# Changing the order of the first batch, and moving one tile's neighbour sums to GpSimd, in a one-core stencil and feed-forward kernel

## The reference

```python
lap_x = (yp_x[:, :, :-2] - 2.0 * y + yp_x[:, :, 2:])      # reflect padding
lap_y = (yp_y[:, :-2, :] - 2.0 * y + yp_y[:, 2:, :])
y = zX * lap_x + zY * lap_y + zR * x * (1.0 - x)          # zX, zY, zR: one number per batch
lt = y[:, 1:17, :]; even, odd = lt[:, ::2, :], lt[:, 1::2, :]
m1 = (even[:, :4, :, None] * odd[:, :4, None, :]).reshape(B, H, D)
m2 = (even[:, 4:, :, None] * odd[:, 4:, None, :]).reshape(B, D, H)
h = einsum('bsd,hd->bsh', y, W1) + scale * einsum('bsd,bhd->bsh', y, m1) + b1
h = gelu(h, approximate=False)
out = x + einsum('bsh,oh->bso', h, W2) + scale * einsum('bsh,boh->bso', h, m2) + b2
```

## Time and profile before

| | us |
|---|---|
| median of 3 runs | 1356.17 |
| lowest and highest | 1356.12, 1356.93 |
| the profiled execution, its own time | 1355.59 |
| span of the profiled execution | 1353.8 |
| TensorE busy in the span | 1341.1 (99%) |
| VectorE, ScalarE, GpSimd busy | 1046.3, 806.7, 420.7 |
| first product of layer 1 | starts at 34.10 |
| first product of layer 2 | starts at 47.63 |

### The profile page before, as it was taken

The page is one execution under the profiler, slowest core; times in us unless marked ns, Lnnn a source line. Parts: engine busy times, 40 slices in busy tenths (PEclk is TensorE's granted clock), DMA queues, the critical chain, the costliest instruction groups (busy, mean ns, idle before and its releaser), DMA issues.

```text
span 1353.8 us, 17005 instructions
## 1 busy us (share of the span) xinstructions
PE 1341.1 (99%) x5840; PEld 1096.2 (81%) x5840; DVE 1046.3 (77%) x1676; ACT 806.7 (60%) x1396; POOL 420.7 (31%) x399
## 2 busy tenths in 40 slices
PE   8899999999999999999999999999999999999999
PEld 4688888888888888888888888888888888888887
DVE  6999889957799577995889768897688967675353
ACT  3766467754676456764567555675466754666432
POOL 3453134511445014450244302453025520222100
PEclk9999999999999999999999999999999999999999
DMA  6688778867687677776778757787677866676661
GB/s 190 157 200 231 229 178 216 209 181 203 190 217 206 181 207 199 208 201 206 198 191 206 190 194 210 196 216 184 212 201 191 217 182 209 151 199 163 179 188 53
DMA packets 134070, 262.04 MB, mean 194 GB/s; under 512 B 15200, under 2 KB 23520, under 8 KB 133984
## 3 DMA queue, kind: packets, MB, share of 16 engines
q1 hardware_dynamic: 116248, 210.36, 48.6%
q0 software_dynamic: 17520, 49.81, 22.7%
q10 hardware_dynamic: 216, 0.79, 0.2%
HBM read 193.80 MB, written 67.11 MB: 193 GB/s over the span
## 4 chain that ended last, share of the span: by engine, by line
PE 93%; DVE 5%; DMA 0%; issue 0%; ACT 0%; SPq 0%; DVEq 0%; ACTq 0%
PE po L471 17%; PE po L472 17%; PE po L473 16%; PE ph L454 14%; PE ph L456 14%; PE ph L458 14%; DVE W2s L439 1%; DVE yl L299 1%; DVE W2l L446 1%; PE po L274 1%; DMA x<-in_xT_dram 0%; DVE gl L489 0%; DVE y L282 0%; DVE W1l L384 0%; DVE y L288 0%
## 5 line engine op out<-in xcount | busy, mean ns | idle before, releaser
L471 PE MATMUL po<-W2h,gh 128*128 128x512 f32 x1024 | 398.5, 389 | 2.8 <-DVE gl L489 2.8
L473 PE MATMUL po<-W2h,gl 128*128 128x512 f32 x1024 | 398.6, 389 | 0.0
L472 PE MATMUL po<-W2l,gh 128*128 128x512 f32 x1024 | 398.6, 389 | 0.0
L454 PE MATMUL ph<-yh,W1h 128*128 128x512 f32 x898 | 351.2, 391 | 2.4 <-DVE W1l L384 1.7
L456 PE MATMUL ph<-yl,W1h 128*128 128x512 f32 x898 | 349.9, 390 | 0.0
L458 PE MATMUL ph<-yh,W1l 128*128 128x512 f32 x898 | 349.8, 390 | 0.0
L489 DVE TENSOR_TENSOR gl<-ph,gh 128x512 fp32r<-128x512 f32 x256 | 175.4, 686 | 188.0 <-ACT gh L487 188.0
L471 PEld LDWEIGHTS po<-W2h,gh 128*128 128x128 f32 x1024 | 192.4, 188 | 43.2 <-DVE gl L489 3.2
L484 ACT ACTIVATE ph<-ph,b1t 128x512 f32<-128x512 f32 x256 | 167.7, 655 | 96.7 <-DVE ph L551 68.7
L473 PEld LDWEIGHTS po<-W2h,gl 128*128 128x128 f32 x1024 | 192.3, 188 | 40.2
L472 PEld LDWEIGHTS po<-W2l,gh 128*128 128x128 f32 x1024 | 192.2, 188 | 39.6
(11 more groups left out here) (91 smaller groups left out, 1285.0 us busy)
## 6 DMA issues: line engine op xcount, KB each, us to landing
W2s<-in_w_dram SPq DMA_DIRECT2D x128, 256.0 KB, 3.2
R<-in_w_dram POOLq DMA_DIRECT2D x63, 512.0 KB, 7.5
uv_scratch<-UVs SPq DMA_DIRECT2D x126, 256.0 KB, 4.4
UVs<-uv_scratch SPq DMA_DIRECT2D x126, 256.0 KB, 3.9
X<-in_xT_dram SPq DMA_DIRECT2D x56, 390.0 KB, 4.5
xr<-in_x_dram SPq DMA_DIRECT2D x16, 1024.0 KB, 5.7
xr<-in_b_dram POOLq DMA_DIRECT2D x16, 1024.0 KB, 11.3
out_dram<-xr SPq DMA_DIRECT2D x64, 256.0 KB, 2.1
```

The costliest lines, as they stand in the source:

```text
L454: e.matmul(bank[:, :], W1h[:, f, blk, wc], yh[:, s, c, :], start=first and c == 0, stop=False, skip_group_check=not first)
L471: e.matmul(po[t][:, :], gh[:, late, st], W2h[:, k, :], start=first, stop=False)
L472: e.matmul(po[t][:, :], gh[:, late, st], W2l[:, k, :], start=False, stop=False)
L473: mm = e.matmul(po[t][:, :], gl[:, late, st], W2h[:, k, :], start=False, stop=last)
```

## The change

Tile 5 joins the tiles whose neighbour sums GpSimd makes: `by_pool` gets 5, and `s0` has a fifth pair of buffers for it. The numbers of `zt` are loaded by ScalarE's queue instead of SyncE's, ahead of the natural rows; the first x tile becomes SyncE's first DMA, and the order of the other loads changes. The products of tile 0 stand ahead of the 20 small warming products (L587). `scalars(0, ...)` is planned earlier. The other lines change planned times of batch 0's first half; they move instructions, as the rows under the diff show, and change nothing in what is computed.

```diff
-            s0 = early.enter_context(nc.sbuf_tensor("s0", [128, 4, 2, 512], f32))
+            s0 = early.enter_context(nc.sbuf_tensor("s0", [128, 5, 2, 512], f32))
...
-        k_z = d_z.dma(sp, us(0.0), [(zt[:, :, :].rearrange("p b i -> p (b i)"),
+        k_z = d_z.dma(act, us(0.0), [(zt[:, :, :].rearrange("p b i -> p (b i)"),
...
-        k_N = d_N.dma(act, us(0.0), [(N, bass.AP(x.tensor, 0, [[S * D, 8], [2 * D, 8], [D, 3], [1, D]]))])
-        k_zn = d_zn.dma(sp, us(0.1), [(zn[:, 0:4], bass.AP(z.tensor, 0, [[4, 8], [0, 8], [1, 4]]))])
+        k_N = d_N.dma(act, us(0.1), [(N, bass.AP(x.tensor, 0, [[S * D, 8], [2 * D, 8], [D, 3], [1, D]]))])
+        k_zn = d_zn.dma(sp, us(0.3), [(zn[:, 0:4], bass.AP(z.tensor, 0, [[4, 8], [0, 8], [1, 4]]))])
...
-                s, pair = n, s0[:, n // 4 * 2 + n % 2, :, :]
-                load = us((0.2, 0.25, 2.1, 0.6, 1.6, 1.7, 1.5, 1.8)[n])
-                adds = us((0, 0, 8.1, 15.4, 0, 0, 6.9, 11.4)[n])
+                s, pair = n, s0[:, (0, 0, 0, 1, 0, 4, 2, 3)[n], :, :]
+                load = us((0.2, 0.6, 0.2, 0.5, 1.7, 1.8, 1.6, 1.9)[n])
+                adds = us((0, 0, 8.8, 20.6, 0, 16.7, 17.1, 17.6)[n])
...
-            by_pool = b > 0 or n in (2, 3, 6, 7)
+            by_pool = b > 0 or n in (2, 3, 5, 6, 7)
...
-                at = us((5, 9.6, 14.9, 0, 17.8, 22.3, 0, 26.8)[n])
+                at = us((-18, 10.2, 12.5, 0, 16, 21.6, 0, 28.6)[n])
...
-                return ((-43.6, 3.2, 12.5), (-49.2, 17.5, 37.3), (45.7, 64.4, 58.8), (63.9, 81.5, 89.5), (95.8, 123.1, 122.2), (120.7, 136.9, 139),
-                        (150.9, 176.2, 167.9), (173.3, 191.3, 184.4))[n]
+                return ((-48.7, -39.2, 12), (-50.1, 16.8, 57.5), (45.2, 63.9, 83.4), (77, 89.4, 89.5), (121.9, 129.5, 130), (128.5, 136.6, 142.1),
+                        (165.6, 179, 174.5), (172.6, 182.4, 211.2))[n]
...
-        scalars(0, us(10.1))
+        scalars(0, us(6.9))
```

More of the change, by code:

```diff
@@ L237, in stencil @@
             if b == 0:
-                s, pair = n, s0[:, n // 4 * 2 + n % 2, :, :]
-                load = us((0.2, 0.25, 2.1, 0.6, 1.6, 1.7, 1.5, 1.8)[n])
-                adds = us((0, 0, 8.1, 15.4, 0, 0, 6.9, 11.4)[n])
+                s, pair = n, s0[:, (0, 0, 0, 1, 0, 4, 2, 3)[n], :, :]
+                load = us((0.2, 0.6, 0.2, 0.5, 1.7, 1.8, 1.6, 1.9)[n])
+                adds = us((0, 0, 8.8, 20.6, 0, 16.7, 17.1, 17.6)[n])
                 adds = (adds, adds + 6)
-                mul, fin = us((5.7, 10, 12.2, 7.6, 17.2, 9.9, 10.9, 21.1)[n]), us((9.8, 15, 16.8, 14.7, 22.6, 28, 17.9, 28.1)[n])
-                fin = (fin, fin + 8.6, fin + 11.9)
+                mul, fin = us((3.7, 11.5, 10.8, 7.7, 23.4, 12.7, 10.9, 13.2)[n]), us((8.5, 11.5, 16.1, 6.6, 24.4, 26.8, 11.8, 25.1)[n])
+                fin = (fin, fin + 47.3, fin + 52.5)
                 free_x, free_y, prev = [], [], None
@@ L307, in operands @@
             else:
-                w0, w1_, w2_, w3, w4 = (us(21.1), us(21.6)), (us(20.8), us(24.4)), (us(37.5), us(43.7)), (us(34.8), us(39.2)), (us(38), us(45.2))
-                ws1, ws2, ws3, ws4 = us(29.1), us(34.7), us(38.4), us(38.2)
+                w0, w1_, w2_, w3, w4 = (us(21.7), us(23.1)), (us(23.8), us(24.2)), (us(45.2), us(44.2)), (us(35.8), us(39.3)), (us(45.4), us(46))
+                ws1, ws2, ws3, ws4 = us(28.9), us(34.8), us(45.6), us(37.7)
             left, hi = [ytile.at(b, n) for n in range(4)], [ytile.at(b, n) for n in range(4, 8)]
@@ L323, in operands2 @@
             T = t0(b, 0, 0)
-            w5, w6 = ((T - 14.6, T + 10.7), (T + 67.8, T + 72.5)) if b else ((110.6, 166), (125.6, 136))
+            w5, w6 = ((T - 14.6, T + 10.7), (T + 67.8, T + 72.5)) if b else ((109.9, 221.8), (124.6, 192.5))
             parts(b, w5, 5, A21, p7.at(b - 1, 7), addS.at(b, "S3"))
@@ L332, in w1_plain @@
             k = d_t[0].dma(sp, us(2.2), [(raw.rearrange("p a q -> p (a q)"), w1[0])])
-            m = pe.put(us(14), lambda e: e.matmul(ph[2][:, 0:256], DG[0:64, 2, :], N[:, 0, 0:256],
+            m = pe.put(us(12.3), lambda e: e.matmul(ph[2][:, 0:256], DG[0:64, 2, :], N[:, 0, 0:256],
                                                   start=True, stop=True), m_ep, m_sel)
@@ L337, in w1_plain @@
                 blk = R1[:, 0, 2 * h:2 * h + 2, 128 * c:128 * c + 128]
-                o = dve.put(us(15.8 + 0.1 * cd), lambda e, cd=cd, blk=blk: e.scalar_tensor_tensor(
+                o = dve.put(us(16.4 + 0.1 * cd), lambda e, cd=cd, blk=blk: e.scalar_tensor_tensor(
                     blk, ph[2][:, 0:256].rearrange("p (a q) -> p a q", a=2), SC[:, 0, cd, 0:1], blk, ALU.mult, ALU.add),
@@ L341, in w1_plain @@
             outer[0, 0] = o
-            stU[0, 0] = stV[0, 0] = d_us[0].dma(sp, us(21.4), [(UV[0, h], raw[:, 2 * h:2 * h + 2, :]) for h in range(2)], o)
-            a = act.put(us(15.1), lambda e: e.activation(W1h[:, 0, 0:3, :], raw[:, 1:4, :], ACT.Copy), o)
-            loB[0, 0] = dve.put(us(19.1), lambda e: e.tensor_tensor(
+            stU[0, 0] = stV[0, 0] = d_us[0].dma(sp, us(19.3), [(UV[0, h], raw[:, 2 * h:2 * h + 2, :]) for h in range(2)], o)
+            a = act.put(us(17.4), lambda e: e.activation(W1h[:, 0, 0:3, :], raw[:, 1:4, :], ACT.Copy), o)
+            loB[0, 0] = dve.put(us(18.2), lambda e: e.tensor_tensor(
                 W1l[:, 0, 0:3, :], raw[:, 1:4, :], W1h[:, 0, 0:3, :].bitcast(f32), ALU.subtract), a)
-            a = act.put(us(16.2), lambda e: e.activation(W1h[:, 0, 3, :], raw[:, 0, :], ACT.Copy))
-            loT[0, 0] = tops[0, 0] = dve.put(us(23.2), lambda e: e.tensor_tensor(
+            a = act.put(us(20.4), lambda e: e.activation(W1h[:, 0, 3, :], raw[:, 0, :], ACT.Copy))
+            loT[0, 0] = tops[0, 0] = dve.put(us(22.9), lambda e: e.tensor_tensor(
                 W1l[:, 0, 3, :], raw[:, 0, :], W1h[:, 0, 3, :].bitcast(f32), ALU.subtract), a)
@@ L354, in w1_pair @@
             if b == 0 and i in (1, 2, 3):
-                w = ((-73.7, -56.5, -36.4, -17.9, -15.1, 1.1, 5.7, -5.9, 13.7, 12.5, 40.2), (-26.6, -27.9, -15.1, 48.6, 63.9, 76.7, 65.1, 51, 73, 67.6, 77.6),
-                     (-11.5, 33.7, 51.1, 99.2, 103.3, 119.7, 113.7, 103.8, 103.3, 126.9, 139.1))[i - 1]
+                w = ((-72.7, -55.2, -38.4, -16.7, -13.8, 2.6, 5.2, -10.3, 17.5, 12.9, 32.1), (-27, -27.8, -18.7, 48.8, 50.4, 76.4, 64.5, 48.2, 71.1, 64.7, 76.4),
+                     (-7.6, 48, 50.6, 105.8, 107.7, 125, 114, 91.9, 103, 127.5, 140.3))[i - 1]
             back = outer.at(b, i - 1) if i else outer.at(b - 1, 7)
@@ L523, in half0_plain @@
             p3[0, 0] = product(T + 18, second, 0, 1, yh0, yl0, 1, False)
-            gelu(0, 0, 0, 0, first, (T + 14.9, T + 18.8, T + 47.2), m)
-            gelu(0, 0, 0, 1, second, (T + 26.4, T + 32.7, T + 46.5), p3.at(0, 0))
+            gelu(0, 0, 0, 0, first, (T + 27.4, T + 28.6, T + 45.3), m)
+            gelu(0, 0, 0, 1, second, (T + 27, T + 33.2, T + 56.1), p3.at(0, 0))
         def half1_plain():
```

## The result

The kernel after takes 1359.54 us in the median of 12 executions (1358.91 to 1360.10), the kernel before 1355.95 beside it: 1.0026, interval 1.0018 to 1.0034. That is 3.6 us slower (forecast: 1.1 us slower), and 0.1 us above the upper end of the forecast range. The profiled execution has a span of 1357.7 us against 1353.8.

The account below looks back on a forecast made before the run. VectorE's stream to about 87 us was taken as the bound. Its terms summed to -0.6 (fold at 82.4); ScalarE's order then made TensorE 1.15 later: 1357.3 us against the median 1356.17, range 1353.4 to 1359.4.

Parts of the forecast that it names:

- Natural rows: Start of VectorE's stream: the natural rows' load, behind `zt`, lands at 8.0 instead of 7.7, costing VectorE 0.3 us.
- rival B: Slower: natural rows land at 9.5, shifting VectorE 1.5 us more; 1358.8, or 1359.4 with GpSimd meetings at their upper end; chance 0.20.
- L204 to L207, +1.3: VectorE's natural-row operations: tile 2's two GpSimd sums now run beside them and cost 1.3 us, between 0 and 2.3.
- The 2.58 us idle go: VectorE's wait before 15.84 for tile 0's products vanishes, since tile 3's first step and the scalars stand ahead: -2.6 us.
- The scalars, +2.2: The six scalars on VectorE: the sixth and L287 now each wait for most of a GpSimd sum; +2.2, between 0 and 2.3.
- The rest up to that fold: VectorE up to W2 tile 7's last fold: two L299 moved behind -2.3, smaller wait -1.0, meetings with GpSimd +1.5.
- -1.0 for the gap: VectorE's 2.27 us wait before 52.77 shrinks to about 1.3 spread over small waits: -1.0 us.
- +1.5 for meetings: VectorE operations waiting for GpSimd's sums in a new pattern, up to W2 tile 7's last fold: +1.5, between -1 and +3.
- Two L299 have gone behind it, -2.3: Two L299 of batch 0's second half, 1.15 us each, stand behind W2 tile 7's last fold: VectorE reaches it 2.3 earlier.
- Where the gain is lost: ScalarE near 83: L444, waiting for the fold, precedes L510; TensorE goes on at 83.5 instead of 82.03, net +1.15 us.
- First layer 2 product 1 to 3 us earlier: TensorE's product at 47.63 starts 1 to 3 us earlier, as VectorE operations move behind the L489 that releases layer 2.
- The clock: TensorE in the first 60 us: a second drop of its granted clock would add up to 1.7 us.

Follow-up runs that it names:

- the front: Kernel after with the later-planned lines (operands, W1 pairs 1 to 3, W2 tiles, first GELU) of the kernel before: 1357.83 us, 1.0017.
- the later tables: Kernel before with only the kernel after's planned times for operands, W1 pairs 1 to 3, W2 tiles and first GELU: 1359.63 us, 1.0023.
- a mend at that place: Kernel after with L298 and L299 of the third operand moved ahead (1.0015), or GpSimd's two sums moved behind VectorE's last L299 of the half (1.0013).
- the repeat: Kernel after, unchanged, measured again beside the kernel before: 1359.86 us, 1.0029.

## Why the prediction was wrong

The sign was right and the size was not: 1.1 us slower was forecast, 3.6 measured. The rest is which terms were mis-sized.

**The bound: right.** VectorE's stream sets most of the time (the L287 of the table), and operations with all data in the common memory wait for GpSimd's sums.

**Natural rows, "I take 8.0", +0.3: too small.** L200 starts at 8.80 instead of 7.73, so +1.1, above the bound of 8.6. It was no chance of one execution: L200 starts between 7.73 and 8.16 in the twelve profiles with the old loads, and between 8.69 and 9.01 in the eight with the new ones. This is rival B's mechanism, at somewhat over half its size. The skill's rule on completion marks (Trainium skill, DMA: Bandwidth & Descriptors, section Queues, rings and completion order) held: VectorE's first step on `zt` starts at 6.07 instead of 3.81. It is issued by the other queue at the same moment as x tile 0 (both at 0.82), not behind it as the prediction has it; x tile 0 landed at 5.77, `zt` at 6.05. The times were not those of the prediction, since the x tile took 4.9 us and not 6.5: tile 0's products, held by the diagonals as the first row of TensorE's waits shows, start at 6.79 and not at 8.

**L204 to L207, +1.3: 2.3**, the upper end. **The 2.58 us idle go: right. The scalars, +2.2: wrong sign.** From L287 (16.50) to the sixth scalar's end took 6.14, against 6.57 before from L282 (15.84). Up to the sixth scalar the sum was +0.2, better than the +1.2 forecast. Up to that point the forecast did not fail, though the front is not free: alone it costs 0.17%.

**"The rest up to that fold" is.** This is the term that failed: behind the sixth scalar I had -1.0 for the gap and +1.5 for meetings, so +0.5. The fold ends at 84.08 instead of 82.98, so +1.1; less the +0.2 of the front and the -2.3 of the two L299 moved behind it, the term measures +3.2. To L287 it is 3.9 - 0.2 = +3.7.

What the traces show in its place: the gap before 52.77 was taken for free time. In it GpSimd has its operations, and the change put the L299 there: 3.90 us, with TensorE waiting for it. Of the seven profiles with the later tables and without a mend at that place, all seven show it (3.90 to 4.28); of the nine with the old tables, where this L299 starts just ahead of GpSimd's L264, only two do (5.42 and 5.45). Near 89 us the L446 came to stand beside three GpSimd operations in the same way. That the later tables alone cost 0.23% is shown. That these two rows are what they cost is not: taking the first away gave between nothing and 2 us, and the second was not tried. How the +3.7 divides stays open.

**"Two L299 have gone behind it, -2.3": the wrong measuring point.** They are moved, not saved. The fold came at 84.08 (forecast 82.4, before 82.98); from its end to L287 it takes 14.1 us instead of 11.3. The run with that line alone shows no gain (1.0002, interval 0.9993 to 1.0011).

**"Where the gain is lost", L510: a symptom.** It did wait as described (84.65; forecast 82.9), TensorE went on at 85.29 (forecast 83.5), and taking the wait away gave nothing.

**The range: too narrow by its own terms.** Rival B is 1358.8 with the meetings at 1.5; with them at their upper end of 3 it is 1358.8 + 1.5 = 1360.3, and not the 1359.4 at which the range stops. The measured time lies below that.

**First layer 2 product 1 to 3 us earlier: no.** 47.66, as before, 46.66 in the repeat.

**The clock: named as a danger, and none.** Two drops happened (0.88 in both windows above), and the repeat without any is no faster.

## To carry over

Where two engines exclude each other, a gap of one can be the other's turn: of the two gaps here one was free (filling it gave 2 us) and one was not. Look at what the other engine does there before you count the gap as free. Measure an order of steps at a point that has the same set of operations behind it in both versions; a step put behind the point is not a gain. Of this change one part is worth keeping: the scalars ahead of tile 0's join, 2.0 and 2.4 us faster than the kernel before in two measurements.
